# The last doubling of the power tables on GpSimd in a state-space stage

## The reference

```python
def s4d(x, log_dt, A_re, A_im, C_re, C_im, D_skip):
    Bb, L, D = x.shape                      # L = 4096, D = 512, 64 states
    dt = jnp.exp(log_dt)
    A = A_re + 1j * A_im
    C = C_re + 1j * C_im
    dtA = dt[:, None] * A
    dC = C * (jnp.exp(dtA) - 1.0) / A
    powers = jnp.exp(dtA[:, :, None] * jnp.arange(L))
    K = 2.0 * jnp.einsum('dn,dnl->dl', dC, powers).real
    n = 2 * L
    Kf = jnp.fft.rfft(K, n=n, axis=-1)
    xf = jnp.fft.rfft(x, n=n, axis=1)
    y = jnp.fft.irfft(xf * Kf.T[None], n=n, axis=1)[:, :L]
    return y + x * D_skip
```

## Time and profile before

| | |
|---|---|
| median of 3 runs | 3927.72 us (3921.81 to 3928.78) |
| span of the profiled execution | 3923.9 us |
| TensorE busy | 3188.6 us, 81% |
| VectorE busy | 2978.2 us, 76% |
| ScalarE busy | 2267.9 us, 58% |
| GpSimd busy | 1587.3 us, 40% |
| the state-space stage | from 1989.2 to 2494.2 us |

### The profile page before, as it was taken

The page is one execution under the profiler, slowest core; times in us unless marked ns, Lnnn a source line. Parts: engine busy times, 40 slices in busy tenths (PEclk is TensorE's granted clock), DMA queues, the critical chain, the costliest instruction groups (busy, mean ns, idle before and its releaser), DMA issues. The chain is left out here.

```text
span 3923.9 us, 54505 instructions
## 1 busy us (share of the span) xinstructions
PE 3188.6 (81%) x17202; PEld 2121.8 (54%) x17202; DVE 2978.2 (76%) x7467; ACT 2267.9 (58%) x2921; POOL 1587.3 (40%) x1268
## 2 busy tenths in 40 slices
PE   7638768777887587877987787689999999958999
PEld 3314334444443344445865555477777777746776
DVE  7799999999999999986679998434444334469888
ACT  4579678888987788882133333133323232347876
POOL 0025556555555466555500000113332323217775
PEclk9868878888888788878999999899999999989999
DMA  8710000000000000002223333643444442330212
GB/s 318 260 42 10 10 8 10 10 12 10 10 10 10 8 10 10 12 5 90 93 54 90 83 93 83 188 129 124 129 131 129 129 129 89 113 119 15 62 54 69
DMA packets 262025, 290.53 MB, mean 74 GB/s; under 512 B 53264, under 2 KB 175782, under 8 KB 260588
## 3 DMA queue, kind: packets, MB, share of 16 engines
q1 hardware_dynamic: 243964, 259.49, 21.9%
q10 hardware_dynamic: 14736, 12.89, 1.0%
q0 software_dynamic: 3040, 14.94, 1.0%
HBM read 218.82 MB, written 68.45 MB: 73 GB/s over the span
## 5 line engine op out<-in xcount | busy, mean ns | idle before, releaser
L1119 PE MATMUL up<-ctx,attnT 128*128 128x384 f32 (+1 forms) x1664 | 717.2, 587 | 45.5 <-ACT attnT L989 45.5
L1089 PE MATMUL score<-KT,q 64*128 64x512 f32 (+1 forms) x1792 | 380.2, 518 | 336.9 <-ACT S L949 246.2
L850 DVE MAX8 both_wide<-S 128x8 f32<-128x146 f32 (+1 forms) x2816 | 601.2, 295 | 44.0 <-ACT S L949 24.7
L809 POOL TENSOR_TENSOR S<-S 128x512 f32<-128x512 f32 (+1 forms) x224 | 424.6, 1928 | 355.1 <-DVE S L855 355.1
L1119 PEld LDWEIGHTS up<-ctx,attnT 128*128 128x128 f32 (+1 forms) x1664 | 366.1, 231 | 322.0 <-issue 162.5
L855 DVE SCALAR_TENSOR_TENSOR S<-S,both_wide 128x3202 f32<-128x3202 f32 x128 | 472.8, 3757 | 14.6 <-ACT both_wide L980 14.6
L1089 PEld LDWEIGHTS score<-KT,q 64*128 64x128 f32 x1792 | 172.3, 235 | 535.1 <-ACT S L949 399.9
L949 ACT ACTIVATE S<-score 128x1024 f32<-128x1024 f32 (+1 forms) x448 | 402.7, 931 | 90.3 <-PE score L1089 90.0
L2242 DVE TENSOR_TENSOR ff_gelu<-ff_whole,ff_gelu 128x512 fp32r<-128x512 f32 x128 | 100.5, 785 | 426.6 <-ACT ff_gelu L2436 426.6
L958 ACT ACTIVATE both_wide<-S,below 128x3202 bf16<-128x3202 f32 x128 | 379.7, 2967 | 43.3 <-DVE below L890 22.5
L980 ACT ACTIVATE both_wide<-S,ebias 128x3202 f32<-128x3202 f32 x128 | 376.3, 2964 | 23.9 <-DVE S L855 13.5
(11 more groups left out here) (435 smaller groups left out, 5982.4 us busy)
## 6 DMA issues: line engine op xcount, KB each, us to landing
s_hankel<-scratch_K SPq DMA_DIRECT2D x128, 256.0 KB, 4.4
ff_w_low<-scratch_w1l SPq DMA_DIRECT2D x112, 256.0 KB, 2.6
ff_w_low<-scratch_w2l SPq DMA_DIRECT2D x112, 256.0 KB, 2.7
xt_prep<-in_x SPq DMA_DIRECT2D x8, 1024.0 KB, 8.5
scratch_xt<-xt_prep SPq DMA_DIRECT2D x8, 1024.0 KB, 8.1
both_wide<-in_ffn_w_t POOLq DMA_DIRECT2D x8, 1024.0 KB, 11.0
q<-scratch_qt SPq DMA_DIRECT2D x128, 64.0 KB, 1.9
mod_xt<-in_x_turned SPq DMA_DIRECT2D x32, 256.0 KB, 2.6
```

The lines of the kernel that those rows point to most:

```text
L809: nc.gpsimd.tensor_tensor(S[:, b, 0, chunk(j)], S[:, b, 0, chunk(j)], S[:, b, 1, chunk(j)], ALU.add).then_inc(s["summed01"], 1)
L850: nc.vector.max(cand[:, h, 8 * k:8 * k + 8], S[:, b, h, k * SEG:min((k + 1) * SEG, G)])
L1089: last = nc.tensor.matmul(score[bank(p, j)][:, e, 0:w], lhsT=q[at, b, part, h // 2, :], rhs=KT[at, h // 2, chunk(j)], start=(part == 0), s ...
L1119: last = nc.tensor.matmul(up[:, 0:DV], lhsT=attnT[0:w, e, c - 4 * g, :], rhs=ctx[0:w, c, :], start=(c == 0), stop=(c == GC - 1))
```

## The change

- VectorE's table(g) makes levels 0 to 5 only (columns up to 63, and column 128), and signals Q_low.
- GpSimd has a new function upper_half(g) that makes columns 64 to 127 in 8 steps of UPPER = 8 columns: two products, into the table itself and into a new tile crossed, a drain, a difference and a sum in place, a drain. It waits for Q_low and signals Q_upper, for which gather(g) on TensorE waits from part 2 on.
- GpSimd's order becomes first_weights, chunk_turn(0), upper_half(2), upper_half(3); then for G = 1 to 6 upper_half(2G + 2), chunk_turn(G), upper_half(2G + 3); then chunk_turn(7).
- The kernel weights of parts 1 to 15 are written by ScalarE, behind the copy into Krow of the part before.
- The bfloat16 identity is no longer made at the program's head and kept throughout, but is made by GpSimd at the head of feed_forward.

```diff
+    UPPER = 8
+        crossed = sb("s4_crossed", [P, 2, GP, UPPER])
...
-                def kernel_weights(g):
+                def first_weights():
 
                     pool.drain()
-                    if g:
-                        pool.wait_ge(s["K_done"], g)
                     for part in range(2):
                         for e in range(2):
                             at = slice(NS * e, NS * (e + 1))
                             last = nc.gpsimd.tensor_scalar(Kz[at, part, :, e:e + CHUNKS * (SIDE - 1) + 1:CHUNKS],
-                                                           root[at, part, pairs(g)].rearrange("p (r j) -> p r j", j=SIDE),
+                                                           root[at, part, pairs(0)].rearrange("p (r j) -> p r j", j=SIDE),
                                                            -1.0 if part else 1.0, None, ALU.mult)
...
+                def upper_half(g):
+
+                    table, at, half = Q[g % RING], pairs(g), P // 2
+                    pool.wait_ge(s["Q_low"], g - 1)
+                    for first in range(0, half, UPPER):
+                        source, to = table[:, :, :, first:first + UPPER], table[:, :, :, half + first:half + first + UPPER]
+                        for part, into in ((0, to), (1, crossed[:])):
+                            nc.gpsimd.tensor_tensor(into, source, W[:, LEVELS - 1, part, at].unsqueeze(1).unsqueeze(3).broadcast_to([P, 2, GP, UPPER]), ALU.mult)
+                        pool.drain()
+                        nc.gpsimd.tensor_tensor(to[:, 0], to[:, 0], crossed[:, 1], ALU.subtract)
+                        last = nc.gpsimd.tensor_tensor(to[:, 1], to[:, 1], crossed[:, 0], ALU.add)
+                        pool.drain()
+                    last.then_inc(s["Q_upper"], 1)
+
                 pool.drain()
-                kernel_weights(0)
+                first_weights()
                 chunk_turn(0)
-                for g in range(1, PARTS):
-                    kernel_weights(g)
-                    if g % 2 and g > 1:
-                        chunk_turn(g // 2)
+                upper_half(2)
+                upper_half(3)
+                for G in range(1, PARTS // 2 - 1):
+                    upper_half(2 * G + 2)
+                    chunk_turn(G)
+                    upper_half(2 * G + 3)
+                chunk_turn(PARTS // 2 - 1)
...
-                    for level in range(1, LEVELS):
+                    for level in range(1, LEVELS - 1):
...
-                    last.then_inc(s["Q_ready"], 1)
+                    last.then_inc(s["Q_low"], 1)
...
-                dve.sem_inc(s["Q_ready"], 2)
...
+                def kernel_weights(g):
+
+                    for part in range(2):
+                        for e in range(2):
+                            at = slice(NS * e, NS * (e + 1))
+                            last = nc.scalar.activation(Kz[at, part, :, e:e + CHUNKS * (SIDE - 1) + 1:CHUNKS],
+                                                        root[at, part, pairs(g)].rearrange("p (r j) -> p r j", j=SIDE),
+                                                        ACT.Copy, scale=-1.0 if part else 1.0)
+                    last.then_inc(s["Kz_ready"], 1)
...
+                    if g + 1 < PARTS:
+                        kernel_weights(g + 1)
                     copy_states(g, UG - 1)
...
-                    pe.wait_ge(s["Q_ready"], g + 1)
+                    if g >= 2:
+                        pe.wait_ge(s["Q_upper"], g - 1)
...
+                nc.gpsimd.tensor_copy(ident_bf[:], const["ident"][:]).then_inc(s["ident_bf_made"], 1)
                 nc.gpsimd.memset(edge[:], 0.0)
...
-                nc.gpsimd.tensor_copy(const["ident_bf"][:], const["ident"][:]).then_inc(ident_made, 1)
-                pool.wait_ge(ident_made, 2)
```

More of the change, by code:

```diff
@@ L1468, in s4d @@
         s = {n: sem("s4_" + n) for n in (
-            "skip_in", "row_set", "Kz_ready", "Q_ready", "turned", "QT_ready", "U_done", "UT_ready", "U_turned", "U_copied", "turn_ready",
+            "skip_in", "row_set", "Kz_ready", "Q_low", "Q_upper", "turned", "QT_ready", "U_done", "UT_ready", "U_turned", "U_copied", "turn_ready",
             "K_done", "K_row", "K_stored", "h_in0", "h_in1", "h_in2", "h_in3", "h_used", "S_ready", "y_done", "yT_ready", "y_turned",
@@ L1923, in feed_forward @@
         zero = sb("ff_zero", [P, DC], BF16)
+        ident_bf = sb("ff_ident_bf", [P, P], BF16)
         edge = sb("ff_edge", [1, 1])
@@ L1938, in feed_forward @@
             "out_wanted", "out_ready", "out_normed", "x_ready", "x_wanted", "x_root", "x_read", "q_ready", "q_turned", "qT_ready",
-            "xt_free", "qT_stored", "rowstep_stored", "x_stored", "x_shifted", "biased", "edges", "rowstep_ready", "rowstep_turned", "rowstep_row", "passed")}
+            "xt_free", "qT_stored", "rowstep_stored", "x_stored", "x_shifted", "ident_bf_made", "biased", "edges", "rowstep_ready", "rowstep_turned", "rowstep_row", "passed")}
         def low_loads(F):
@@ L2529, in turn_q @@
                     n = QUAD * g + k
+                    if n == 0:
+                        pe.wait_ge(s["ident_bf_made"], 1)
                     pe.wait_ge(s["q_ready"], n + 1)
@@ L2538, in turn_q @@
                         last = nc.tensor.transpose(fl[k % 2 if g == QUADS - 1 else 1][:].bitcast(BF16)[:, c * P:(c + 1) * P], q[:, k, c * P:(c + 1) * P],
-                                                   const["ident_bf"][:])
+                                                   ident_bf[:])
                     last.then_inc(s["q_turned"], 1)
@@ L3151, in xattn_ffn @@
         const = {"ident": sb("ident", [P, P]), "ones": sb("ones", [P, 1]),
-                 "eps": sb("eps", [P, 1]),
-                 "ident_bf": sb("ident_bf", [P, P], BF16)}
+                 "eps": sb("eps", [P, 1])}
         ident_made = sem("ident_made")
```

## The result

The changed kernel takes 4023.6 us in the median of 4 runs (4021.3 to 4025.7), where 3925.35 us (3921.8 to 3928.8, 4 runs) stood: 1.0251 times as long, with a 95% interval of 1.0237 to 1.0266. That is 98.3 us more. The forecast was 4045.3 us, within 4003 to 4090.

The account below looks back on a forecast made before the run. VectorE was taken as the state-space stage's bound, TensorE close behind. Start 100 + five cycles of 81.0 + 56 + end 61.6 = 622.6 us against 505.0, +117.6: span 4041.5, time 4045.3 us, range 4003 to 4090.

Parts of the forecast that it names:

- The chain: State-space steady cycle: carry waits for chunk_turn behind upper(2G+2), next odd table behind carry; 75.4 us before overlap, against 61.7.
- X: GpSimd's time for one table's last doubling in the state-space stage: 8 x 2.42 = 19.4 us.
- The lock in the chain: GpSimd's delay from overlap with VectorE's lower levels: between 0 and 11.2 us, taken as 5.6 us a cycle.
- the start: State-space stage until table(4) is complete: between 91 and 115 us, taken as 100 us.
- from table 14 to table 15: Last stretch between complete tables in the state-space stage: 56.0 us, with no overlap.
- the end: State-space stage from the start of gather(15) to the store of y: stays 61.6 us.
- the step on the lock: Overlap in the state-space stage: engines take turns by whole instructions; VectorE's delay in a cycle costs nothing, GpSimd's 5.6 us.
- the sign: In the profile after, VectorE's largest wait is the carry's for chunk_turn, 25 to 35 us in each of six cycles.
- The forecast for VectorE's busy time: State-space stage: VectorE busy some 115 us less than 426.9 us.
- TensorE's near tie: Steady cycle: TensorE's two gathers and spread take 45 us against 44 us to carry's end; not a second chain.
- the rival's turning point: Rival of a faster kernel, 3886 us, chance 0.05: needs a GpSimd step below 1.57 us, X below 12.6 us.
- The small parts: Kernel weights on ScalarE, -0.2 to +0.5 us a cycle, and the moved identity cast, within 0.5 us: both taken as 0.

Follow-up runs that it names:

- the run without lower levels: The changed kernel with levels 2 to 5 of the even tables from table 4 on left out on VectorE: 4002.0 us, 1.0198.
- carry split: The changed kernel with chunk_turn issued ahead of upper_half(2G+2), and VectorE's two-part carry split into one-part carries after each table: 3963.5 us, 1.0099.
- side work: The kernel before, with GpSimd doing 8 steps of same-shaped work that nobody waits for, for each part from 2 on; identity cast moved: 4054.1 us, 1.0324.
- one low table: No separate run: the lower levels of table 10 on VectorE in the changed kernel, beside GpSimd, 18.9 us instead of 11.0.
- the first and the fourth run: Changed kernel with chunk_turn ahead of upper_half(2G+2), 4006.0 us; changed kernel with only odd tables' last doubling on GpSimd and chunk_turn ahead, 4009.0 us.
- table 2 into modulate: The kernel before with table 2 formed whole by GpSimd in the stage modulate, VectorE beginning with table 3: 3914.3 us, 0.9971.

## Why the prediction was right, and where it was not

**The chain: right.** The step that the carry waits for chunk_turn, chunk_turn stands behind upper(2G+2), and table(2G+3) behind the carry, is what the four windows show: 1.9 + 22.9 + 11.0 + 19.1 + 22.1 us. X was forecast as 19.4 from the step of modulate and is 19.1. (By the rule of the Trainium skill, GPSIMD Engine Reference, section Engine selection, about twice VectorE's time, it would have been an estimated 16.4; the trace has 2.3 times.)

**The lock in the chain: mis-sized.** It was put at half of the range, 5.6 us a cycle; the trace and the run without lower levels give 3.0. With 0.3 us less for each upper half, 0.2 for the lower levels and 0.5 for the handovers, the cycle is 77.1 where 81.0 stood: 5 x 3.9 = 19.5 of the 21.8 us by which the stage was forecast too long (622.6 against 600.8). The other terms: the start 101.4 instead of 100, from table 14 to table 15 55.0 instead of 56.0, and the end 59.1 instead of 61.6. The last one goes with the granted clock, 0.95 in the last window of the stage where it was 0.87. The kernel after, and the kernel before:

```profile
2555.00:2591.30 36.30, 23.84 (x492) 14.06 (x484) 9.42 (x36) 6.24 (x11) 0.00 (x0) 0.95 0.84 217
```

```profile
2455.00:2493.80 38.80, 25.69 (x480) 14.77 (x480) 9.30 (x35) 6.25 (x11) 0.00 (x0) 0.87 0.80 204
```

**What the step on the lock missed.** It said that VectorE's own loss costs nothing since it waits for chunk_turn anyway. That holds in the steady cycle of the changed kernel, and only because of the chain. (The loss of 7.9 us is also most of why the wait for chunk_turn is 24.2 us and not the 25 to 35 that was named as the sign.) The experiments show that it is the larger price: 0.39 us (carry split), 0.48 (side work) and 0.50 (one low table) of VectorE's time for each microsecond of GpSimd's. A last doubling takes 8.2 us on VectorE and 19.1 on GpSimd; moved, it costs VectorE 19.1 x 0.39 to 0.48 = 7.4 to 9.2 us in lost turns. So of the 8.2 us next to nothing is freed. With the split carry it is at most 0.9 us a table: the cycle of 69.4 us stands against an estimated 61.7 + 9.5 = 71.2 for the kernel before with the same split, which was not run. The forecast for VectorE's busy time, some 115 us less, failed for the same reason: it fell by 56, since time in which an instruction is held up counts as busy. Five overlaps of 7.9 us, and 16.5 us at the start (VectorE is done with carry(1) 71.3 us in, not 54.8), make up 56 of the missing 59.

**What was missed altogether.** TensorE's near tie was seen, but only as a check on spread. The ring gather, carry of both parts, lower levels, upper half was not in the prediction, though the carry's wait for the gathered inputs of both parts stands in the description of the kernel. It does not move the forecast, being 1.3 us shorter than the ring that was in it; that the forecast did not suffer from it is luck. It does make the rival's turning point wrong. I put it at a step of 1.57 us, by the ring through chunk_turn and without VectorE's loss. By the second ring, carry 22.9, lower levels 11.0 and gather 19.0 leave 8.8 of the 61.7 us for an upper half, an estimated step of 1.1 us. The expectations for the first and the fourth run repeat the miss, by 66 and 72 us.

**The small parts** were right: kernel weights on ScalarE make no measurable difference. The cast of the identity was not tried by itself; the program behind the stage, where it now lies, kept its length within 0.1 us.

What stays open is how the two shares of the 98 us divide. In the changed kernel they do not simply add: where the chain makes VectorE wait, its loss to the blocking is hidden. No kernel here has the two engines side by side in this stage without the blocking.

## What to carry to other kernels

Before moving elementwise work from a full VectorE to GpSimd, look at what runs on VectorE at that time: where it is two-input work on SBUF, 0.4 to 0.5 of GpSimd's time came back here as a loss of VectorE, and with GpSimd 2.3 times slower next to nothing was left of the gain. Move it to a stage where GpSimd's step is known to be free, as table 2 into modulate. And when a queue's new order closes a ring through two engines, follow every wait of the waiting instruction, not only the latest one: the carry had two, and the second ring was 1.3 us behind the first.

## What the runs showed of the hardware

Short two-input instructions hold each other up as the long ones of the earlier trace rows do. A GpSimd product of 128x256, 0.64 us alone, takes up to 1.09 beside VectorE's; a VectorE product of 128x512 has a mean of 892 or 810 ns, by the table, instead of 687. In modulate, a VectorE instruction with one SBUF tensor as input kept its 746 to 750 ns beside GpSimd's. (The Trainium skill, SBUF — State Buffer, section Who interferes with whom: only the port pair that the two share causes contention, as an exclusive lock, and a VectorE instruction with two SBUF inputs contends with a GpSimd one that reads SBUF. The trace agrees; it adds that between streams of short instructions VectorE loses 7.9 us while GpSimd loses 3.0 in the same 18.9 us.) The loss has no wait in the profile and no idle time: only the durations, read by shape against a kernel without the overlap, show it.
